# One region of instructions for all four stages, and the rows of the first expert stage added inside latent attention

## The reference, cut to what matters

```
x = x + 0.5 * lora_moe(layernorm(x))        # 8 small experts, top 2
x = x + attention(layernorm(x))             # 16 heads of 16
x = x + 0.5 * lora_moe(layernorm(x))
x = x + 0.5 * experts(layernorm(x))         # 32 experts, 4 for each row      (stage "m1")
x = x + latent_attention(layernorm(x))      # 16 heads, causal, low rank q/kv (stage "a1")
x = x + 0.5 * experts(layernorm(x))         # the same weights and routing     (stage "m2")
```

## Time and profile before

| | |
|---|---|
| three timed runs | 1598.66, 1597.33, 1587.52 us; median 1597.33 |
| the profiled execution's own time | 1589.9 us |
| span of the profile | 1588.1 us |
| mean granted clock of PE | 0.875 of full speed |
| busy: PE, DVE, ACT, POOL | 77%, 58%, 41%, 36% of the span |
| first layer | 0 to 581 us |
| m1: blocks, then rows added | 581 to 757, to 803 us |
| a1: opening, steps, last rows | 803 to 842, to 1345, to 1379 us |
| m2: blocks, then rows added | 1379 to 1546, to 1588 us |

### The profile page before, as it was taken

The page is one execution under the profiler, slowest core; times in us unless marked ns, Lnnn a source line. Parts: engine busy times, 40 slices in busy tenths (PEclk is TensorE's granted clock), DMA queues, the critical chain, the costliest instruction groups (busy, mean ns, idle before and its releaser), DMA issues. The chain is left out here.

```text
span 1588.1 us, 20981 instructions
## 1 busy us (share of the span) xinstructions
PE 1216.4 (77%) x5912; PEld 749.3 (47%) x5912; DVE 916.4 (58%) x2601; ACT 648.9 (41%) x1706; POOL 568.9 (36%) x621
## 2 busy tenths in 40 slices
PE   4778888748868428999237989988988998299990
PEld 2432333213223316888124545745655655288870
DVE  6677567527744402223747877797698794122227
ACT  2114444424536114555113654455355453055550
POOL 1054532543453144555002121143134133355550
PEclk8787988868979759999658999999999999699995
DMA  3654670560221345554600000000001011344547
GB/s 107 108 92 108 163 174 37 94 166 21 76 85 37 125 177 176 159 160 146 215 14 1 1 1 1 1 30 24 1 13 42 1 71 37 132 153 160 160 135 269
DMA packets 81761, 145.73 MB, mean 92 GB/s; under 512 B 15396, under 2 KB 63685, under 8 KB 78837
## 3 DMA queue, kind: packets, MB, share of 16 engines
q1 hardware_dynamic: 62133, 102.02, 23.4%
q0 software_dynamic: 17408, 42.00, 7.5%
q10 hardware_dynamic: 2112, 0.38, 0.1%
HBM read 81.11 MB, written 63.00 MB: 91 GB/s over the span
## 5 line engine op out<-in xcount | busy, mean ns | idle before, releaser
L138 POOL DMA_INDIRECT outs_dram<-m_ys,dest x192 | 184.7, 962 | 175.5 <-ACT m_ys L996 161.1
L753 DVE TENSOR_REDUCE a_mx<-a_psU 128x1 f32<-128x512 f32 x256 | 164.8, 685 | 135.6 <-PE a_psU L384 126.4
L1338 ACT ACTIVATE a_pr<-a_psA,a_nb 128x512 f32<-128x512 f32 (+3 forms) x256 | 132.8, 525 | 239.3 <-DVE a_nb L1455 233.2
L1016 DVE TENSOR_TENSOR m_hm<-m_psG,m_sg 128x128 f32<-128x128 f32 x192 | 56.1, 292 | 293.0 <-ACT m_sg L990 176.5
L1060 PE MATMUL m_psG<-arena,m_xgT 128*128 x768 | 207.2, 393 | 0.6 <-issue 0.2
L1394 POOL TENSOR_TENSOR a_q<-a_q,a_t 64x512 f32<-64x512 f32 x64 | 81.1, 1267 | 342.5 <-DVEq L1450 328.8
L536 ACT ACTIVATE a_P<-a_psS 128x512 f32<-128x512 f32 x256 | 143.2, 596 | 106.6 <-PE a_psS L395 84.8
L138 POOL DMA_INDIRECT rows_dram<-a_xd,slot x128 | 125.3, 979 | 120.7 <-DVE a_xd L124 51.3
L1060 PEld LDWEIGHTS m_psG<-arena,m_xgT 128*128 128x128 f32 x768 | 134.1, 195 | 16.9 <-issue 4.5
L384 PE MATMUL a_psU<-arena 96*128 96x512 bf16 x256 | 108.2, 430 | 35.3 <-DVE a_mx L753 33.8
L1051 PE MATMUL m_psX<-ident,m_xg 128*128 128x128 f32 x384 | 75.2, 280 | 71.5 <-DMA m_xg<-rows_dram 71.5
(11 more groups left out here) (246 smaller groups left out, 2168.5 us busy)
## 6 DMA issues: line engine op xcount, KB each, us to landing
m_xg<-rows_dram SPq DMA_DIRECT2D x48, 512.0 KB
arena<-in_mo_w SPq DMA_DIRECT2D x8, 2048.0 KB
arena<-part_dram SPq DMA_DIRECT2D x96, 128.0 KB
rows_dram<-arena SPq DMA_DIRECT2D x12, 1024.0 KB
m_xg<-outs_dram SPq DMA_DIRECT2D x16, 512.0 KB, 4.4
m_ys<-outs_dram SPq DMA_DIRECT2D x16, 512.0 KB, 4.8
part_dram<-a_part SPq DMA_DIRECT2D x16, 384.0 KB
outs_dram<-m_ys,dest POOLq DMA_INDIRECT x192
```

The costliest lines, as they stand in the source:

```text
L138: pool.indirect_dma_start(out=rows_dram, out_offset=bass.IndirectOffsetOnAxis(ap=slot[:, c:c + 1], axis=0), in_=row, in_offset=None).then_ ...
L753: dve.tensor_reduce(mx[g % 2][:, 4 * kt + qt:4 * kt + qt + 1], psU[n % 2][:, :], AX, ALU.max).then_inc(u_free, 1)
L1338: ins = act.activation(pr[S % 2][:, AT[t]:AT[t] + (t + 1) * P], psA[:, AT[t]:AT[t] + (t + 1) * P], ACT.Exp, bias=nb[S % 2][:, t:t + 1], sc ...
```

## The change

All stages share one region; the drains and barriers at the ends of the first layer, m1 and a1 go, and the waits that were always in the code order the stages instead. Semaphores of all stages live until the end. m1 no longer adds its results to x. Latent attention does: DVE adds tiles 0 to 3 before the opening and one more tile at the end of twelve steps (`ADD_AT`), and makes statistics, scales and normalised rows of one batch at a time (`first_rows`), for the next batch at s = 5. SP loads the result rows from the queue of a1 into the fourth chunk of `arena`, whose weights are loaded again once tile 15 is added, so that m2 waits for nine loads and not eight. The tables of side units move: `x` from s = 1, 2 to 6, 7; `o` from 3 to 6 to 2 to 5; `d` from 7, 8 to 8, 9; `qT` from 12 to 13; `k` from 13, 14 to 14, 15; norms and rotary product of the keys one step later. PE waits before the first scores of a batch for the copy of its last key unit.

```diff
@@ first_layer, moe_stage, latent_stage: no region of their own
-        block = ctx.enter_context(nc.Block())
@@ moe_stage, sync and vector: only m2 (result given) still loads and adds
+            if result is not None:
+                for t in range(TILES + NP):
...
-            for t in range(TILES):
+            for t in range(TILES if result is not None else 0):
...
-                if result is None:
-                    dve.wait_ge(added, (t + 1) * TOPK)
-                    dve.bn_stats(r.stats[:, 6 * t:6 * t + 6], xt)
@@ latent_stage
-    X_AT, O_AT, D_AT, Q_AT, K_AT = (1, 2), (3, 4, 5, 6), (7, 8), 12, (13, 14)
-    LN_AT, STATS_AT, SCALES_AT, XD_AT, NORMS_AT, ROPE_AT = 0, 6, 7, 8, 9, 10
+    X_AT, O_AT, D_AT, Q_AT, K_AT = (6, 7), (2, 3, 4, 5), (8, 9), 13, (14, 15)
+    LN_AT, STATS_AT, SCALES_AT, XD_AT, NORMS_AT, ROPE_AT = 5, 6, 7, 8, 10, 11
+    NP, ADD_AT = 4, {0: 4, 1: 5, 2: 6, 3: 7, 6: 8, 8: 9, 11: 10, 14: 11, 17: 12, 20: 13, 24: 14, 28: 15}
+    PREPARED = H1 + PAIRS + 2
...
             def scores(h, k):
+                if k == 0 and h % H1 == 0:
+                    pe.wait_ge(u_free, u_index[("k", h // H1, 1)] + 1)
...
         def _(sp):
+            for t in range(TILES):
+                if t >= NP:
+                    sp.wait_ge(added, (t - NP + 1) * TOPK)
+                sp.dma_start(pk[t % NP], picked_rows(out_dram, t)).then_inc(picked[t % NP], 16)
+            (first, first_src), (low, low_src), (high, high_src) = reloads
+            sp.wait_ge(added, TILES * TOPK)
+            sp.dma_start(first, first_src).then_inc(experts_in, 16)
...
-            row_scales(dve, link, r)
+            def add_rows(t):
+                xt = x[:, t * D:(t + 1) * D]
+                dve.wait_ge(picked[t % NP], 16 * (t // NP + 1))
+                for c in range(t * TOPK, (t + 1) * TOPK):
+                    if c % TOPK:
+                        dve.wait_ge(added, c)
+                    dve.scalar_tensor_tensor(out=xt, in0=pk[t % NP][:, c % TOPK * D:(c % TOPK + 1) * D], scalar=half_weight[:, c:c + 1],
+                                             in1=xt, op0=ALU.mult, op1=ALU.add).then_inc(added, 1)
+            def first_rows(b):
+                dve.wait_ge(added, (b + 1) * TPB * TOPK)
+                link(row_stats(dve, r, b))
+                scales(b, 0, TPB)
+                normal_rows(dve, x, b, mv, rstd, 0, xn, xn_ready)
...
-            layernorm(dve, r, 0, xn, xn_ready)
+            for t in range(TPB):
+                add_rows(t)
+            dve.wait_ge(la.kept, PREPARED)
+            first_rows(0)
...
+                if S in ADD_AT:
+                    add_rows(ADD_AT[S])
                 if s == LN_AT and b + 1 < B:
                     made(dve, ("x", b, 1))
-                    layernorm(dve, r, b + 1, xn, xn_ready)
+                    first_rows(b + 1)
@@ program: the one region, and the chunk for the result rows
+        block = ctx.enter_context(nc.Block())
...
-            latent_stage(nc, r, ident, la, slot, rows_dram, placed[1], arena[:, 4 * half:], early, experts_in)
-        moe("m2", placed[1], 8, None, (xv, written))
+            latent_stage(nc, block, sem, r, ident, la, slot, rows_dram, placed[1], arena[:, 4 * half:],
+                         arena[:, 3 * half:4 * half], weight, outs_dram, [load(3)] + early, experts_in)
+        moe("m2", placed[1], 9, None, (xv, written))
```

More of the change, by code:

```diff
@@ L143, with first_layer @@
 GROUPS = B * H // HPG
-def first_layer(nc, r, ident, ring, wt, wmain, wlora, iota, bias_qk, bias_v, bias_o, part_dram, slot, rows_dram,
+def first_layer(nc, block, sem_of, r, ident, ring, wt, wmain, wlora, iota, bias_qk, bias_v, bias_o, part_dram, slot, rows_dram,
                 placed, early, middle, late, experts_in, weight, block_expert, dest, dest_in, table_dram, spare, first_loads,
@@ L903, in _, with picked_rows, moe_stage @@
                 sp.dma_start(dst, src).then_inc(experts_in, 16)
-def moe_stage(nc, tag, r, ident, weights, weights_in, slot, half_weight, block_expert, rows_dram, placed,
+def picked_rows(out_dram, t):
+    return out_dram[t * P * TOPK:(t + 1) * P * TOPK, :].rearrange("(p k) d -> p (k d)", k=TOPK)
+def moe_stage(nc, block, sem_of, tag, r, ident, weights, weights_in, slot, half_weight, block_expert, rows_dram, placed,
               out_dram, dest, dest_in, latent, result):
@@ L930, in moe_stage @@
                              "h_turned", "hT_ready", "y_done", "y_copied", "added"))
-        made, kept = sem("made"), sem("kept")
+        made, kept = sem("made"), latent.kept if latent is not None else None
         block_in = [sem(f"block_in{i}") for i in range(NX)]
@@ L957, in _ @@
                 sp.wait_ge(saved[n], 16 * (NBLK // NY))
[L958 to L966, removed]
-            if result is not None:
-                sp.wait_ge(result[1], 16 * TILES)
+            if result is not None:
+                out, written = result
+                for t in range(TILES + NP):
+                    if t >= NP:
+                        sp.wait_ge(added, (t - NP + 1) * TOPK)
+                    if t < TILES:
+                        sp.dma_start(pk[t % NP], picked_rows(out_dram, t)).then_inc(picked[t % NP], 16)
+                    if t >= NP:
+                        sp.dma_start(out[:, t - NP, :], x[:, (t - NP) * D:(t - NP + 1) * D]).then_inc(written, 16)
+                sp.wait_ge(written, 16 * TILES)
         @block.gpsimd
@@ L1005, in _ @@
                     act.copy(la.vo[:, c * D:(c + 1) * D], (psX + psG)[c % 4][:, 0:D]).then_inc(kept, 1)
-                act.copy(la.identb[:, :], ident[:, :])
-                act.copy(la.mask[:, :], la.maskf[:, :])
+                act.copy(la.identb[:, :], ident[:, :]).then_inc(kept, 1)
+                act.copy(la.mask[:, :], la.maskf[:, :]).then_inc(kept, 1)
         @block.vector
@@ L1165, in sem @@
         def sem(n):
-            return ctx.enter_context(nc.semaphore(f"a1_{n}"))
+            return sem_of(f"a1_{n}")
+        pk = [picks[:, i * TOPK * D:(i + 1) * TOPK * D] for i in range(NP)]
+        added, picked = sem("added"), [sem(f"picked{i}") for i in range(NP)]
         part = spare.shape[1] // 2
@@ L1624, in program @@
         arena = sb("arena", [P, NE * (KD * 2 * INTER + D)])
-        experts_in, latent_in, written, dest_in = (sem(n) for n in ("experts_in", "latent_in", "written", "dest_in"))
+        experts_in, latent_in, latent_kept, written, dest_in = (sem(n) for n in (
+            "experts_in", "latent_in", "latent_kept", "written", "dest_in"))
         placed = [[sem(f"m{m}_placed{i}") for i in range(2)] for m in (1, 2)]
@@ L1649, in program @@
         moe = lambda tag, placed, loads, latent, result: moe_stage(
-            nc, tag, r, ident, arena[:, :], (experts_in, 16 * loads), slot, weight, block_expert, rows_dram, placed,
+            nc, block, sem, tag, r, ident, arena[:, :], (experts_in, 16 * loads), slot, weight, block_expert, rows_dram, placed,
             outs_dram, dest, dest_in, latent, result)
```

21 lines of the change are left out of this document (10 added, 11 removed).

## The result

The changed kernel takes **1574.64 us** (median of four runs, 1573.10 to 1577.26); the kernel before, now with a fourth run, 1597.90 (1587.52 to 1598.66). The ratio is **0.9871, 95% interval 0.9828 to 0.9914**. In a later comparison with more runs it came out at 0.9883 (0.9854 to 0.9911). The forecast of 1576.6 us is a ratio of 0.987.

A forecast was written before the change was run, and what follows sets the result against it. DVE was taken to set plain steps and the stretch behind m1, PE the steps with an output product. Barriers and rows -38.9, steps +18.2, together -20.7 us: 1576.6 us against the median, range 1561 to 1597.

The forecast's parts named there:

- steps: Latent attention's 64 steps: batch 0 +12.9, batch 1 +3.9, batch 2 -1.6, batch 3 0, key copy's wait +3.0; +18.2 us.
- barrier after the first layer: End of the first layer: SP waits for the scatters itself, so the next loads start 3.1 us earlier.
- barrier ahead of m2: Between latent attention and m2: SP waits for the scatters itself, so m2's first load starts 5.7 us earlier.
- normalised rows of batch 0: Start of latent attention: rows need only four added tiles, ending at 778.7 instead of 808.84 us; gain 30.1 us.
- batch 3: Last batch of latent attention's steps: only the output products move by one step, cost 0.
- key copy's wait: Before a batch's first scores PE waits for the last key copy; 1.0 us each, three times, +3.0 us.
- adds at S = 8 and 20: Adds in steps with 1.7 and 1.8 us of room: forecast to cost 0 and +0.3 us.
- Nothing covered: Rival, chance 0.18: in the steps' ring of DVE, ACT and PE all 37.5 us come back; -1.4 us, 1596.
- better covered: Rival, chance 0.10: the engine chain has more room in the steps, half of the 18.2 falls away; -30, 1567 us.
- Barriers give nothing: Rival, chance 0.06: at stage ends what SP waits for comes only as the drain ends, 8.8 us lost; -12, 1585.
- slower: Rival, chance 0.07: DVE-bound steps idle PE, its clock falls to 1.2 GHz in batches 0 and 1; +18.6, 1616 us.
- Lock: Rival, chance 0.04: each of twelve adds in the steps waits out POOL's 1.25 us, +15; so -6, 1591 us.

The follow-up runs named there:

- before_again: The kernel before, unchanged, run again for a second profile; median 1592.35 us.
- one_region_only: The kernel before with all stages in one region of instructions, rows and side-unit tables as before; 1585.85 us, ratio 0.9935 to the kernel before.
- change_again: The change, unchanged, run again in a later session; 1580.10 us, ratio 0.9883 to the kernel before.
- adds_in_room: The change with adds of tiles 8 to 15 moved to steps where DVE was idle 2.0 to 4.3 us; 1568.51 us, ratio 0.9826 to the kernel before.
- adds_in_gaps: The change with tiles 4 to 11 added in the opening's DVE waits, 12 to 15 at S = 9, 13, 15, 19; 1561.37 us, ratio 0.9779 to the kernel before.
- regions_back: The change with one region of instructions for each stage again, adds still inside latent attention; 1586.62 us, ratio 0.9963 to the kernel before.

## Why the prediction came out

The two large parts, the barriers and the rows of batch 0, came out by their mechanism. That the steps' +18.1 meets +18.2 so exactly is luck, as the parts below show. Terms of the sum, in us, change minus before; for the steps the means of the profiles of each (before: the first profile, before_again and one_region_only; change: the first profile and change_again):

| term | forecast | measured |
|---|---|---|
| barrier after the first layer | -3.1 | -3.13 |
| barrier ahead of m2 | -5.7 | -5.76 |
| normalised rows of batch 0 | -30.1 | -30.39 |
| steps | +18.2 | 492.1 - 474.0 = +18.1 |
| sum | -20.7 | -21.1 |

The medians differ by 23.3 us, the two ratios say 20.6 and 18.7. Single pairs of these profiles give 13.5 to 21.3 us for the steps, so their exact sum is also an accident of the clock in each.

- **The bound was read rightly**: which engine sets a step is told by its own window, not by the stage's busy share. What a DVE-set step gets, it pays in full: 1.96 us for a tile of four adds, and S = 0 to 3 took 7.8 to 7.9 us.
- **Inside the steps** the parts were: batch 0 forecast +12.9, measured +14.2 (131.3 against 117.1); batch 1 +3.9, +3.3; batch 2 -1.6, -1.8; batch 3 0, **+2.4**. The miss in batch 3 is the step "only the output products move by one step, 0": at the old place the last product covered four statistics, and a product on an odd step meets the value product. Two of the 2.4 us come back with the old places; the rest is a lower clock at S = 57 of the first profile.
- **The key copy's wait**, +3.0 forecast, is there. In the change ACT copies the last keys at the end of each batch, and PE's first scores of the next start behind the copy. At S = 15:

```profile
949.13 0.62 ACT L1330 COPY a_kT<-a_psU 128x512 f32<-128x512 f32 x1
949.86 1.10 PE L1253 MATMUL a_psA<-a_kT,a_q 128*128 128x512 f32 x2 [1.68 <-issue]
```

  PE idles 1.68 us here, and 1.41 at the same place of S = 31 and 47, and each time the scores start 0.1 us behind the copy's end; the list of waits puts these to "issue" and to POOL and so hides them. Its cost was isolated by no run. The last steps of the three batches grew from 7.96, 8.58 and 8.34 us (before) to 8.80, 9.04 and 9.04 (change_again), 2.0 together, but a key unit moved into them as well, and before the change PE waited 2.16 us for the same copies at the query product.
- **Luck in the sum.** With 1.0 for the key copy in each of batches 0 to 2 the forecast had +13.9, +4.9, -0.6 and 0; measured were +14.2, +3.3, -1.8 and +2.4. Batches 1 and 2 gave back 2.8 us more than forecast, and batch 3 cost 2.4 more. Single places missed too: S = 6 grew by 2.4 us (2.1 forecast), but by the clock and not by its add, and the adds at S = 8 and 20 cost 0.6 and 0.9 instead of 0 and 0.3.
- **Where 30 us went.** Of the 30.4, 7.1 are mostly the statistics and scales of three batches (44.0 to 36.9), and 23.3 are the twelve adds, of which 18 come back. The statistics and scales cost 5.5 us at S = 5 and 2.0 each at S = 21 and 37; together with the moved tables they cost about nothing, since the steps without adds take 474.5 and 473.3 us, where the kernel before has 474.0 in the mean. With the barriers' 8.9 that is the whole gain.
- **The rivals.** *Nothing covered* (+37.5 in the steps) is out by the +18.1, and its mechanism is refuted by adds_in_room; *better covered* needed other places. *Barriers give nothing* and *slower* are out by the terms above, though steps at a low clock and longer for it are real (S = 6, 7 and 18). *Lock* is below.

## What the runs showed of the hardware

**The lock.** In the change one of twelve adds met POOL, at S = 11: four adds 2.33 us instead of 2.04, beside the rotation's products of POOL, one of which took 0.68 us instead of 0.45. In the kernel with adds in full steps, DVE's add and POOL's query sum met at S = 28:

```profile
1068.53 3.06 DVE L1434 SCALAR_TENSOR_TENSOR x<-arena,weight,x 128x256 f32<-128x256 f32 x4
```

```profile
1068.49 1.26 POOL L1397 TENSOR_TENSOR a_q<-a_q,a_t 64x512 f32<-64x512 f32 x1 [1.52 <-DMA rows_dram<-a_xd,slot]
```

```profile
L1434 DVE SCALAR_TENSOR_TENSOR x<-arena,weight,x x4: 485/485/1497, 1068.5 to 1071.1; 128x256 f32<-128x256 f32 x4
```

POOL began 0.04 us ahead. One add of 0.485 us became 1.497, 1.01 us longer, of the 1.22 that the sum still had to run. The Trainium skill (SBUF — State Buffer, Who interferes with whom) says that a DVE instruction with two SBUF inputs contends with a GpSimd instruction that reads SBUF, and that whoever issues first holds the shared pair for its whole instruction: this trace agrees. At the change's places it cost 0.3 us, because the adds stand where POOL's sum is over. In the opening's second gap (adds_in_gaps) sixteen adds took 8.73 us instead of 7.92, beside the same products of POOL.

**A region's end** costs POOL a drain of 2.68 or 5.27 us, or 9.97 at the end of m1. The last one is recorded from before the last scatter is issued (768.1 against 769.21 in regions_back), so the lengths don't compare as they are: from the end of the last scatter's issue to the drain's end it is 4.3, 7.0 and 7.9 us. How these lengths come about was not tried.

**The clock** is granted at 1.2 GHz for part or all of some steps, in some executions of a kernel and not in others. S = 6 follows a step in which PE was busy 8.1 of 10.0 us; it took 7.30 us at 0.77 and 8.25 at 0.54, and the step behind it 8.05 at 1.00 and 9.45 at 0.86. What makes one execution get the one and one the other was not tried.

## What to carry to other kernels

Price an added instruction by the step that it lands in: in a step that its engine sets it costs its whole length or more, in one that another engine sets nothing, and the widest idle stretches may lie ahead of the loop. A barrier costs what the slowest drain has no cover for, so when work is moved away from one, price it again. And compare single steps or single stretches of two profiles, not their ends: ten microseconds came and went here in a stage that no edit touched.
